# One reduction over 1024 columns of scores in place of two over 512, out of one two-bank buffer

## What is computed

```python
q = layernorm(x) @ wq + bq                # (16, 64, 128)
k = ctx @ wk + bk ; v = ctx @ wv + bv     # (16, 1601, 128)
att = softmax(q k^T / sqrt(8))            # per head: 64 x 1601 scores
x = x + (att v) @ wo + bo
# then self attention and a mixture of experts, then layer 1:
# a second cross attention (16 heads of 64), a recurrent block, a feed-forward
```

## Time and profile before

| | |
|---|---|
| median of 3 runs | 2067.46 us (2066.22 to 2070.15) |
| the profiled execution | 2070.69 us, of which the span of the trace is 2068.9 us |
| mean granted TensorE clock | 0.909 of full speed |
| busy, whole span | PE 1746.9, PEld 1232.3, DVE 1276.0, ACT 853.5, POOL 504.4 us |
| L871, the reductions of the side banks | 416, of them 384 of 512 columns and 32 of 260 |
| first cross attention, steps of its 32 octets | 84 to 589 us of the span |

### The profile page before, as it was taken

The page is one execution under the profiler, slowest core; times in us unless marked ns, Lnnn a source line. Parts: engine busy times, 40 slices in busy tenths (PEclk is TensorE's granted clock), DMA queues, the critical chain, the costliest instruction groups (busy, mean ns, idle before and its releaser), DMA issues. The chain is left out here.

```text
span 2068.9 us, 33746 instructions
## 1 busy us (share of the span) xinstructions
PE 1746.9 (84%) x11837; PEld 1232.3 (60%) x11837; DVE 1276.0 (62%) x3092; ACT 853.5 (41%) x1895; POOL 504.4 (24%) x684
## 2 busy tenths in 40 slices
PE   5899999999966666428999999999999999999432
PEld 2466666666655555426666666766667666675322
DVE  5566666666736545636666656666666666654467
ACT  2355555565532122114444444444444444443132
POOL 1000001000001010023442344443234444320133
PEclk9699999999977776768999999999999999999765
DMA  4344435444210020040000000000000000000000
GB/s 104 92 105 105 112 81 113 98 112 106 55 42 1 1 81 0 0 152 27 27 11 27 16 26 26 26 10 26 18 23 26 26 26 10 16 1 1 0 5 5
DMA packets 32628, 90.06 MB, mean 44 GB/s; under 512 B 8552, under 2 KB 17424, under 8 KB 32528
## 3 DMA queue, kind: packets, MB, share of 16 engines
q1 hardware_dynamic: 32528, 88.71, 16.0%
HBM read 40.43 MB, written 8.91 MB: 24 GB/s over the span
## 5 line engine op out<-in xcount | busy, mean ns | idle before, releaser
L1904 PE MATMUL c_pv_ps<-c_prob_t,c_xn 128*128 128x512 f32 (+2 forms) x896 | 413.1, 598 | 0.0
L340 ACT ACTIVATE c_prob<-c_score_ps,c_neg_max 128x512 f32<-128x512 f32 (+1 forms) x512 | 304.3, 607 | 60.4 <-PE c_scratch L1890 35.0
L871 DVE TENSOR_REDUCE a_chunk_max<-a_side_ps 128x1 f32<-128x512 f32 (+1 forms) x416 | 260.7, 664 | 109.5 <-PE a_side_ps L692 109.4
L359 DVE TENSOR_REDUCE c_chunk_max<-c_score_ps 128x1 f32<-128x512 f32 (+1 forms) x512 | 290.9, 581 | 38.1 <-PE c_score_ps L266 36.6
L237 PE MATMUL c_turn_ps<-consts,c_prob 128*128 128x128 f32 (+2 forms) x1792 | 285.7, 276 | 5.2 <-DVE c_prob_t L369 4.3
L237 PEld LDWEIGHTS c_turn_ps<-consts,c_prob 128*128 128x128 f32 (+2 forms) x1792 | 212.4, 139 | 89.2 <-issue 32.4
L1904 PEld LDWEIGHTS c_pv_ps<-c_prob_t,c_xn 128*128 128x128 f32 (+2 forms) x896 | 158.4, 191 | 164.6 <-issue 164.5
L373 DVE COPY c_prob_t<-c_turn_ps 65x128 f32<-65x128 f32 (+1 forms) x256 | 61.5, 280 | 300.5 <-PE c_turn_ps L237 300.5
L804 ACT ACTIVATE a_prob<-a_st_ps 128x1024 f32<-128x1024 f32 (+1 forms) x224 | 214.4, 958 | 66.8 <-PE a_st_ps L676 66.8
L266 PE MATMUL c_score_ps<-c_x_hi,c_q_hi 128*128 128x512 f32 (+1 forms) x512 | 218.8, 427 | 2.4 <-ACT c_prob L340 1.6
L266 PE MATMUL c_score_ps<-c_x_hi,c_q_lo 128*128 128x512 f32 (+1 forms) x512 | 188.6, 368 | 0.0
(11 more groups left out here) (286 smaller groups left out, 2649.9 us busy)
## 6 DMA issues: line engine op xcount, KB each, us to landing
a_stack<-a_k_hi SPq DMA_DIRECT2D x128, 200.1 KB, 4.1
a_stack<-a_k_lo SPq DMA_DIRECT2D x64, 200.1 KB, 4.2
a_ctx<-in_ctx_dram SPq DMA_DIRECT2D x16, 768.0 KB
c_ctx<-in_ctx_dram SPq DMA_DIRECT2D x16, 768.0 KB
absorbed_queries<-b_q_out SPq DMA_DIRECT2D x16, 512.0 KB, 4.7
c_q_raw<-absorbed_queries SPq DMA_DIRECT2D x16, 512.0 KB, 3.3
w<-in_L_ffn_w_dram SPq DMA_DIRECT2D x2, 512.0 KB
f_raw<-in_L_xattn_Wkv_dram SPq DMA_DIRECT2D x2, 512.0 KB, 4.7
```

The lines of the kernel that those rows point to most:

```text
L340: nc.scalar.activation(prob[s % 2][:, cols], score_ps[:, cols], ACT.Exp, bias=neg_max[:, s % 2:s % 2 + 1], accum_out=sums[:, (s // QUAD) % ...
L359: nc.vector.reduce_max(chunk_max[:, s % 2, c:c + 1], score_ps[:, quad_chunk(c, keys)], AX_X).then_inc(chunk_max_done, 1)
L871: nc.vector.reduce_max(out, rows, AX_X).then_inc(side_taken, 1)
L1904: last = nc.tensor.matmul(lay.own.pv_ps[:], t.xn[m][0:rows, i, :], lay.own.prob_t[u][0:rows, i, :], start=(i == 0), stop=(i == LAT))
```

## The change

`side_ps` becomes one tensor of two banks, and a maximum unit now covers two chunks: TensorE writes both banks with two matmuls of 512 columns, one signal follows the second, and VectorE reduces the 1024 columns in one instruction to two numbers. An octet has 6 such units and the short one (`UNITS = 7`). They stand at the same steps as before. Small products and the short unit use the first bank. Since all products share the buffer, each now waits until the product right before it has been taken, not the one two before. `chunk_max` is laid out anew (12 chunk maxima, then 4 for the last keys), and `neg_max` is made by three instructions: a reduction of 12 to 4, a maximum with the last 4, and a multiplication by -1, with a semaphore wait between each two.

```diff
-UNITS = 3 * QUAD + 1
+UNITS = 3 * QUAD // 2 + 1
...
-    return [("max", octet + 1, i) for i in range(2 * at, min(2 * at + 2, UNITS))] if octet + 1 < OCTETS else []
+    return [("max", octet + 1, at)] if octet + 1 < OCTETS else []
...
-    return [("max", 0, i) for i in range(UNITS)] + [("shift", 0)] + [("max", 1, i) for i in range(6)]
+    return [("max", 0, i) for i in range(UNITS)] + [("shift", 0)] + [("max", 1, i) for i in range(3)]
...
-        side_ps = [ctx.enter_context(nc.psum_tensor(f"a_side_ps{i}", [P, BANK], F32)) for i in range(2)]
+        side_ps = ctx.enter_context(nc.psum_tensor("a_side_ps", [P, 2, BANK], F32))
...
-                bank = side_ps[number % 2]
-                if number >= 2:
-                    pe.wait_ge(side_taken, number - 1)
+                bank = side_ps[:, 0, :]
+                if number >= 1:
+                    pe.wait_ge(side_taken, number)
...
-                    if i < 3 * QUAD:
-                        c = i % 3
-                        last = of_pair(bank[:], i // 3, slice(c * BANK, c * BANK + BANK))
+                    if i < UNITS - 1:
+                        for half in range(2):
+                            j, c = divmod(2 * i + half, 3)
+                            last = of_pair(side_ps[:, half, :], j, slice(c * BANK, c * BANK + BANK))
...
-                    if i < 3 * QUAD:
-                        out, rows = chunk_max[:, i // 3, i % 3:i % 3 + 1], bank[:]
+                    if i < UNITS - 1:
+                        out, rows = chunk_max[:, 2 * i:2 * i + 2], side_ps[:]
...
-                        nc.vector.tensor_reduce(neg_max[:], chunk_max[:], AX_X, ALU.max, negate=True).then_inc(neg_done, 1)
+                        nc.vector.tensor_reduce(pair_max[:], chunk_max[:, 0:3 * QUAD].rearrange("p (j c) -> p j c", c=3), AX_X, ALU.max).then_inc(pair_done, 1)
+                        dve.wait_ge(pair_done, n + 1)
+                        nc.vector.tensor_tensor(pair_max[:], pair_max[:], chunk_max[:, 3 * QUAD:4 * QUAD], ALU.max).then_inc(pair_all, 1)
+                        dve.wait_ge(pair_all, n + 1)
+                        nc.vector.tensor_scalar(neg_max[:], pair_max[:], -1.0, None, ALU.mult).then_inc(neg_done, 1)
```

More of the change, by code:

```diff
@@ L539, in cross_attention_0 @@
         prob = [sb(f"prob{i}", [P, 2, BANK]) for i in range(3)]
-        chunk_max, neg_max = sb("chunk_max", [P, QUAD, CHUNKS]), sb("neg_max", [P, QUAD])
+        chunk_max, neg_max = sb("chunk_max", [P, 4 * QUAD]), sb("neg_max", [P, QUAD])
+        pair_max = sb("pair_max", [P, QUAD])
         raw = [sb(f"raw{i}", [P, P]) for i in range(2)]
@@ L556, in cross_attention_0 @@
         side_ready, side_taken, neg_done = (sem(n) for n in ("side_ready", "side_taken", "neg_done"))
+        pair_done, pair_all = sem("pair_done"), sem("pair_all")
         pv_taken, heads_done = (sem(n) for n in ("pv_taken", "heads_done"))
@@ L577, in q_bank @@
         def q_bank(i):
-            return (st_ps[1][:, 0, :], st_ps[1][:, 1, :], side_ps[0][:], side_ps[1][:])[i % 4]
+            return (st_ps[1][:, 0, :], st_ps[1][:, 1, :], side_ps[:, 0, :], side_ps[:, 1, :])[i % 4]
         @block.sync
@@ L865, in take_side @@
                         dve.wait_ge(neg_done, n)
-                    if i < 3 * QUAD:
-                        out, rows = chunk_max[:, i // 3, i % 3:i % 3 + 1], bank[:]
+                    if i < UNITS - 1:
+                        out, rows = chunk_max[:, 2 * i:2 * i + 2], side_ps[:]
                     else:
-                        out = chunk_max[:, :, 3]
+                        out = chunk_max[:, 3 * QUAD:4 * QUAD]
                         rows = bank[:, 0:66 * QUAD].rearrange("p (j k) -> p j k", j=QUAD)[:, :, 0:TAIL]
```

## The result

The changed kernel takes **2170.6 us** (median of 4 runs, 2166.2 to 2172.5) against 2067.1 (2066.2 to 2070.2): 1.0495 times as long, 95% interval 1.0474 to 1.0515. The forecast was 2140, the range 2112 to 2165. The direction was right; of the 103 us the forecast had 72, and the time lies above the range.

A forecast was written before the change was run, and what follows sets the result against it. TensorE was taken to bound the changed stage, so its new waits add time: 14 examples x 3.9 = 54.6, plus 9.4 and 8.8 at the edges, less 0.4, is 72.4 us; forecast 2140 us, range 2112 to 2165.

The forecast's parts named there:

- The bound: In the changed stage TensorE, busy 95.25 of 100 us, sets the time; shorter VectorE reductions in themselves give nothing.
- The reduction of 1024 columns at 1.22 us, from 0.65 us after the pair: VectorE's merged reduction waits for both matmuls, begins at 0.65 us and ends at 1.87.
- Rival 3: Not slower: VectorE reads the two banks at once, adding about 2 us at the start alone, 2069 us; chance 0.03.
- Small products 0.75 and 0.53 us later: den and shift each start 0.75 us later in even octets, 0.53 in odd; 2.56 us per example.
- nothing is lost behind `shift`: From shift to weigh_values 1.69 to 1.72 us, against 1.74 before; taken as -0.04 twice.
- Pairs no closer than 2.04 us: Minimum distance between pairs; four shorter distances between steps lose, 1.43 us for an example.
- all four places named: Distances under 2.04 us: steps 5 to 6 in even octets; 0 to 1, 5 to 6, 6 to next 0 in odd.
- Rival 1: Only the small products wait, pairs do not; an example loses 2.5 us, 2116 us in all; chance 0.10.
- The sum for an example: Two octets take 2.56 + 1.43 - 0.08 = 3.9 us more, on 32.5.
- The edges: Loss outside the full examples: 9.4 us ahead of the first octet, 8.8 us in the last four octets.
- rival 2: TensorE's clock falls for a tenth of the stage's 505 us: 33 us more, 2173 us; chance 0.11.

The follow-up runs named there:

- e3: Kernel before, where only the first unit of each two and the short unit wait for the product right ahead of them; 2095.1 us, ratio 1.0141.
- e4: Kernel before, where all products wait as in the kernel after, but reductions stay two of 512 columns, each after its own matmul; 2131.4 us, ratio 1.0317.
- e1: Kernel after, with six useless matmuls added on TensorE right ahead of both den and shift in odd octets; 2140.7 us, ratio 1.0354.
- e2: Kernel before, where only den and shift wait for the product right ahead of them; 2097.6 us, ratio 1.0152.
- e9: Kernel after, with six useless matmuls added ahead of den alone in odd octets; 2163.7 us, ratio 1.0457.
- e6: Kernel after, with the scratch job of a step put ahead of its small product instead of behind it; 2152.9 us, ratio 1.0415.
- e5: Kernel after, with four useless matmuls added ahead of den and shift in even octets, none in odd ones; 2164.1 us, ratio 1.0466.
- e11: Kernel after, with chunk_max laid out as 4 x 4 so that one reduction makes neg_max, as before; 2180.7 us, ratio 1.0534.
- e10: Kernel after, with six useless matmuls added ahead of shift alone in odd octets; 2140.2 us, ratio 1.0357.

## Why the prediction was wrong, point by point

- **The bound.** Right: TensorE's order sets the stage, and what it waits is lost. VectorE's shorter reductions gave nothing.
- **The reduction of 1024 columns at 1.22 us, from 0.65 us after the pair.** Right: 1.223, and 0.66 (328.57 - 327.91). Rival 3, the two banks read at once, is out.
- **Small products 0.75 and 0.53 us later.** Right: 1.94 us after the pair, and idle for 1.19 in place of 0.66. That nothing is lost behind `shift` was right too: it is 1.71 us to `weigh_values` in an undisturbed octet (1.69 to 1.72 worked out).
- **Pairs no closer than 2.04 us.** Right: 2.03 to 2.06 from `weigh_values` to `weigh_values` at all four places named. Rival 1, that only the small products wait, is out: the waits between pairs cost 1.1 to 1.3 us for an example (e3, e4). The sum for an example was 3.9, measured 4.03.
- **The edges.** Too small: the loss up to the first mark was worked out as about 11 us, counting the first octet's own waits, and is 12.7; behind the 27th mark it was about 10 and is 12.4. I carried the rule through in the mean and not step by step.
- So the waits cost 77.5 us where the sum said 72.4. With them alone the kernel takes 2140.7 us (e1), and the forecast was 2140; a part of that agreement is luck, since e1's trace has 5 us less behind the stage.
- **The step that failed is the clock.** The sum took it at 1.00, and rival 2, with the chance 0.11, put the clock's price at 33 us. It costs 25.3 in the stage. I held against it that rows of before show a clock of 1.00 with TensorE busy for 8.39 of 10 us, and 3.62 of 5. The first was a stretch with a dense one right behind (10.00 of 10 us busy from 540 on), and the second ends the stage, with TensorE idle for the next 5 us and the clock at 0.79 in them; neither shows what comes after a thin stretch inside the stage. In the kernel after, 2.81 of 4 us twice was followed by a fall in one example and, with the same figures to 0.01, not in the one before it:

```profile
269.42:273.42 4.00, 2.81 (x40) 1.96 (x28) 2.79 (x4) 1.56 (x3) 0.46 (x1) 1.00 0.02 4
273.42:277.42 4.00, 2.82 (x32) 1.50 (x24) 2.90 (x7) 2.03 (x3) 0.00 (x0) 1.00 0.00 0
277.42:281.42 4.00, 3.38 (x33) 1.99 (x37) 2.31 (x4) 1.94 (x3) 1.03 (x1) 1.00 0.37 77
```

The rows of before bore out that such a stretch can pass, and I read them as if it always did. The Trainium skill (TensorE: Matmul & The Clock Gate, "A second HAM failure mode: psum-queue depth-cycling") says that short idles between groups of matmuls, from cycling through PSUM, can make the clock oscillate. The trace agrees: nine falls, none of them after an idle of more than 1.2 us; e2 has idles as long, and its clock doesn't fall in the loop.
- **The range.** It left out the rival that held. A range up to that rival's price, 2173, would have taken in the result.

Open: why some odd octets are followed by a fall and others, with the same waits to 0.05 us, are not. The falls have an order: in the kernel after and in e9 two examples in a row have a long one and the next two have none, and in e6 it is every third example. What sets this order, no run here shows. The six long falls of the loop keep their places to 1 us in the traces of the kernel after, e5 and e11. Whether their number changes between executions of one kernel isn't shown: there is one trace of each, and the runs of e9 (2154.1 to 2166.5 us) lie no wider than those of the kernel before (2060.5 to 2074.4), which has no falls in the loop of its trace.

## What to carry to other kernels

Two banks that are filled and given back together are one buffer. Merging two reductions saved 0.07 us for each pair on an engine that had time, and cost the engine that had none 3.2 us for the lost overlap and 0.9 for the later start in each example. Where the bound engine works in a fixed order, count for each product that it issues how long after its predecessor it may begin, with every kind of product that shares the buffer, the small ones first; and where new waits thin its work in one place, ask whether work can be put in just there, be it useless: six added matmuls ahead of one wait in each odd octet gave back 25.6 us of the stage (e10, last mark at 667.6 us in place of 693.2).

## What the runs showed of the hardware

- TensorE's clock fell from 2.4 to 1.2 GHz out of stretches in which it was busy for 70% of the time and never idle for more than 1.2 us (kernel after), busy for 3.71 and 3.13 of 4 us (e9), or never idle for more than 0.70 us (e6). It did not fall in e2 with 2.73 and 2.82 of 4 us and idles of 1.27 us. A long fall in the loop of the kernel after cost 3.5 to 3.7 us; TensorE was busy without a gap while the clock was at 0.50 (4.00 of 4 us).
- One reduction of 2 x 512 columns over two PSUM banks takes 1.22 us and two of 512 back to back 1.29: the second instruction, directly behind the first, costs 0.07 us more than its columns in one instruction.
- Three VectorE instructions that write four elements for each partition (the first reads 12), each waiting for the one before by a semaphore, take 0.57 us from the start of the first to the end of the last (84.89 to 85.46 us of the trace), 0.17 each and 0.03 between them.
